# GpSimd's rope sum done head by head, each half with its own count for TensorE's query turn, in an attention and mixture-of-experts layer on one core

## What is computed

```python
norm_q = rmsnorm(x @ W_cq, q_scale)                       # 128 wide
q_nope = (norm_q @ W_dq_nope).reshape(B, S, NH, NOPE)
q_rope = apply_rope((norm_q @ W_dq_rope).reshape(B, S, NH, ROPE), cos, sin)
norm_kv = rmsnorm(x @ W_ckv, kv_scale)                    # 64 wide
scores = concat(q_nope, q_rope) @ concat(k_nope, k_rope / NH) / sqrt(192)
attn = softmax(causal(scores))
x = x + (attn @ value) @ W_o + experts(xn)
```

## Time and profile before

| | |
|---|---|
| median of 3 runs | 1901.81 us (1901.77 to 1904.15) |
| profiled execution | 1908.06 us, span 1906.3 us |
| TensorE busy (PE) | 1479.5 us, 78% |
| VectorE busy (DVE) | 1075.6 us, 56% |
| ScalarE busy (ACT) | 939.0 us, 49% |
| GpSimd busy (POOL) | 647.1 us, 34% |

### The profile page before, as it was taken

The page is one execution under the profiler, slowest core; times in us unless marked ns, Lnnn a source line. Parts: engine busy times, 40 slices in busy tenths (PEclk is TensorE's granted clock), DMA queues, the critical chain, the costliest instruction groups (busy, mean ns, idle before and its releaser), DMA issues. The chain is left out here.

```text
span 1906.3 us, 37123 instructions
## 1 busy us (share of the span) xinstructions
PE 1479.5 (78%) x10111; PEld 1259.3 (66%) x10113; DVE 1075.6 (56%) x4271; ACT 939.0 (49%) x2739; POOL 647.1 (34%) x704
## 2 busy tenths in 40 slices
PE   3662499979799898989989985889998887886340
PEld 2551477767677777777777774678887776775330
DVE  2895266555566555555656653645555666564465
ACT  1330276656566566655666652456666545452000
POOL 1110144434444444444544440000001333334665
PEclk8666699999999999999999997789999889896575
DMA  3992511321311111111111114745455566565553
GB/s 142 341 376 84 226 54 54 127 64 51 143 54 56 53 45 55 61 56 55 41 58 56 46 34 148 248 148 163 150 162 164 182 190 188 181 194 160 158 163 115
DMA packets 169549, 240.44 MB, mean 126 GB/s; under 512 B 16787, under 2 KB 142739, under 8 KB 165011
## 3 DMA queue, kind: packets, MB, share of 16 engines
q1 hardware_dynamic: 146322, 183.61, 29.2%
q0 software_dynamic: 18432, 50.36, 8.5%
q10 hardware_dynamic: 4608, 4.20, 0.8%
HBM read 115.42 MB, written 122.68 MB: 125 GB/s over the span
## 5 line engine op out<-in xcount | busy, mean ns | idle before, releaser
L997 ACT ACTIVATE prob<-prob,negmax 128x512 f32<-128x512 f32 (+3 forms) x512 | 285.5, 560 | 293.4 <-DVE negmax L1073 202.8
L1073 DVE CUSTOM_DVE_ANT_0 prob<-ps,mask_add 128x512 f32<-128x512 f32 (+3 forms) x512 | 248.6, 486 | 240.6 <-issue 237.6
L809 POOL TENSOR_TENSOR qp<-qa,qb 128x512 f32<-128x512 f32 x64 | 81.2, 1269 | 462.5 <-DVE qb L1058 462.5
L61 PE MATMUL ps<-kt_hi,qt_hi 128*128 (+4 forms) x512 | 189.0, 369 | 23.0 <-issue 21.5
L821 POOL DMA_INDIRECT sorted_x<-xn_row,row_no x192 | 188.2, 980 | 48.7 <-issue 44.0
L63 PE MATMUL ps<-kt_hi,qt_lo 128*128 (+4 forms) x512 | 166.8, 326 | 0.0
L62 PE MATMUL ps<-kt_lo,qt_hi 128*128 (+4 forms) x512 | 166.2, 325 | 0.0
L919 PE MATMUL ps<-ident,prob 128*128 128x128 f32 x1280 | 160.7, 273 | 0.0
L935 PE MATMUL ps<-pt,nkv 128*64 128x512 f32 (+3 forms) x1024 | 152.0, 439 | 2.3 <-DVE lat L1091 2.3
L919 PEld LDWEIGHTS ps<-ident,prob 128*128 128x128 f32 x1280 | 143.5, 140 | 0.2 <-ACT prob L997 0.2
L1010 ACT ACTIVATE pt<-ps 128x1024 f32<-128x1024 f32 (+2 forms) x130 | 130.4, 1003 | 14.2 <-PE ps L919 8.7
(11 more groups left out here) (240 smaller groups left out, 4551.4 us busy)
## 6 DMA issues: line engine op xcount, KB each, us to landing
sorted_x<-zeros SPq DMA_DIRECT2D x16, 2048.0 KB, 9.4
rows_in<-sorted_x SPq DMA_DIRECT2D x128, 256.0 KB, 2.8
sorted_y<-rows_out SPq DMA_DIRECT2D x128, 256.0 KB
nqt<-nqt_dram SPq DMA_DIRECT2D x16, 512.0 KB, 3.7
raw_gu<-in_wgu SPq DMA_DIRECT2D x16, 384.0 KB, 4.0
x_in<-in_x SPq DMA_DIRECT2D x8, 512.0 KB, 4.2
xn_dram<-xn SPq DMA_DIRECT2D x8, 512.0 KB, 5.0
xnt_dram<-xnt_hi SPq DMA_DIRECT2D x16, 256.0 KB, 4.7
```

Of the source, the lines that this page charges most:

```text
L61: pe.matmul(out, lh, rh, start=first, stop=False, **kw)
L997: act.activation(prob[:, i, qt, 0:w], prob[:, i, qt, 0:w], ACT.Exp, bias=negmax[:, i, qt:qt + 1], scale=-1.0, accum_out=rowsum[:, g // 2 % ...
L1073: dve.tensor_tensor_reduce(prob[:, i, qt, 0:w], s_ps[k % 2][:, 0:w], mask[:, S - w:S], -1.0, -MASKED, ALU.add, ALU.min, negmax[:, i, qt:qt ...
```

## The change

GpSimd's rope sum of a pair, one instruction over both heads, becomes two, one for each head, and each adds one to `q_done`. TensorE's query turn no longer waits once for the pair; it waits ahead of each head's four transposes for that head's count. Each sum covers 256 elements per partition in place of 512. The wait for `q_abs` stays as it is.

```diff
             def rope_add(b, p):
 
                 pool.wait_ge(q_rope, NP_ * b + p + 1)
-                pool.tensor_tensor(qp[:, :, :, KVR:P], qa[:], qb[:], ALU.add).then_inc(q_done, 1)
+                for i in range(2):
+                    pool.tensor_tensor(qp[:, :, i, KVR:P], qa[:, :, i, :], qb[:, :, i, :], ALU.add)\
+                        .then_inc(q_done, 1)
...
                 pe.wait_ge(q_abs, NP_ * b + p + 1)
-                pe.wait_ge(q_done, NP_ * b + p + 1)
                 for i in range(2):
+                    pe.wait_ge(q_done, NH * b + 2 * p + i + 1)
                     for t in range(TT):
                         mm = pe.transpose(qt_ps[i][:, t * P:(t + 1) * P], qp[:, t, i, :], ident[:])
                     mm.then_inc(qt_ready, 1)
```

## The result

The changed kernel takes 1880.1 us in the median (1875.0 to 1882.0, 4 runs) against 1902.7 (1901.8 to 1904.2, 4 runs) of the kernel before: ratio 0.9876, 95% interval 0.9855 to 0.9898, 22.6 us. The forecast was 12.4 us. The profiled executions differ by more than the medians, 1906.3 to 1879.5 us of span, since the one of the kernel before, 1908.1 us, lay 3.9 us above the highest of its other runs.

The account below looks back on a forecast made before the run. The loop of TensorE's scores, VectorE's chain, GpSimd's sum and the turn was taken to bound the heads stage: 49 x 0.30 = 14.7 us gained, 15 x 0.15 = 2.3 lost, 12.4 net, so 1889.4 us, range 1880 to 1900.

Parts of the forecast that it names:

- (a): GpSimd's rope sum: each half takes 0.73 us, the second ending 1.42 after the sum's start instead of 1.27.
- T: The start of GpSimd's rope sum in a pair, from which the prediction counts its times.
- d: Time the split adds to GpSimd's sum: 0.15 us, with ends at 0 and 0.31.
- The other rule that the prediction weighed: VectorE operations with two SBUF inputs and GpSimd operations exclude each other; the second half reaches 0.15 us further beside VectorE.
- (b): TensorE's query turn: head 0's transposes lie beside GpSimd's second half, so what follows head 1 comes 0.30 us earlier.
- g: Gain per turn from the earlier head 1, 0.45 - d = 0.30 us, in 49 turns.
- (c): Other queues: GpSimd's spread, ScalarE's copies and VectorE's next maximum stay covered, VectorE's idle time shrinking from 1.09 to about 0.8.
- (d): First output pieces: TensorE waits for GpSimd's latent remainder, so 15 of 64 pairs gain nothing and lose 0.15 us each.
- the loop's jumps: Fifth rival: TensorE's gaps there, 7.67 to 1.74 us, can move a few us either way; no separate chance given.
- overlap: First rival: GpSimd's halves overlap, d is 0 to 0.05, gain 18.9 to 22 us, 1880 to 1883; chance 0.08.
- other wait: Third rival: another engine holds TensorE; 1896.8 with half the gain given back, 1902 to 1904 with all; chance 0.14.

Follow-up runs that it names:

- split alone: Changed kernel, but TensorE waits for both halves of the sum before head 0 (also called the kernel with the single wait); ratio 1.0033 to the kernel before.
- swapped waits: Kernel before with only the order of TensorE's waits for `q_abs` and `q_done` ahead of the turn changed, `q_done` first; ratio 0.9967 to the kernel before.
- padded one: Changed kernel with five identity transposes that nobody reads between head 0's and head 1's transposes; ratio 0.9967 to the kernel before.

## Why the prediction was short

The loop that bounds the kernel, VectorE's chain, GpSimd's sum and the turn, was the right one: the plain pairs of the changed kernel, of the split alone and of the swapped waits close on it within 0.01 us once the terms are known, and shortening its next term brought 0.50 a pair more.

(a) held: a half takes 0.730 us (0.73), the second starts 0.69 behind the first, the second ends at T + 1.42, so d = 0.15. The split alone showed it in the pairs with a first piece. That the Trainium skill's GPSIMD Engine Reference, section 2.1, lets a core go on to the next instruction when its share is done gave no more than the 0.04 of overlap that the row had shown; the forecast by the row was right to the hundredth. The other rule that the prediction weighed, on VectorE operations with two SBUF inputs, was not tested: the copy beside the sums reads PSUM alone and the latent product PSUM and one tile in SBUF, so neither is of that kind, and the even times of the sums say nothing on it.

(b) held but for a small term that was mis-sized. TensorE's reaction to the sum, 0.14, was taken from the row of before and carried over to the wait for head 1. In the changed kernel it is 0.05 there, because that wait stands alone ahead of its instruction. That a separate wait costs this much was shown by the swap of two lines. With 0.06 less for it, the gain g of a turn is 0.36, and 40 pairs would bring 14.4 us in place of 12.0 (measured 14.2).

(c) held: VectorE's idle time before the next maximum is 0.74 (about 0.8), and no other engine came up. Two of the prediction's figures were misworked, without weight for the forecast: by its own terms head 0 comes 1.41 - 0.87 = 0.54 us earlier, not 0.57, and d = 0.22 gives 8.0 us, not 7.6.

(d) held: the pairs with a first piece lose 0.14 (0.15), the wait has its row in the trace after, and moving the remainder took it away.

The step that failed is the one on the loop's jumps. I called them a few us either way, which only widened the range, and put them at nothing in the sum beyond their pairs' own share. They and the stage's start brought 10.9 us where the sum had 2.4, of it 6.9 at the four short jumps, where the four pairs' own share is 4 x 0.36 = 1.4. The mean granted clock of the stage, 0.98, hid it, and the first matmul behind the gap doesn't tell: the earlier trace rows gives it 0.79 us at the first jump and 0.50 at the last, but the level behind the last was low as well. The window of the kernel before that begins 0.5 us behind that restart shows it:

```profile
972.52:975.52 3.00, 3.00 (x15) 2.86 (x14) 0.91 (x4) 0.82 (x2) 0.00 (x0) 0.51 0.15 38
```

Such windows behind the jumps could have been read before the forecast. Before and after differ by 1.72 us a short jump, of which 0.36 is the pair. The level there went with the loop's length; the idle time in the turns, the wait in the last turn ahead and the divided wait didn't decide it. Why it goes with the length stays open. For the start, filling the idle time did as much as the change, 2 to 3 us. The long jumps gave 0.9 each; their gaps alone vary between 5.8 and 7.7 us from one to the next and from trace to trace, and that stays open.

Of the rivals, overlap gave nearly the right time (1880 to 1883) for a wrong reason, since d was 0.15 and not 0 to 0.05. No other wait took the place.

## What to carry to other kernels

When one loop sets the time, write its terms from the rows until they close, then divide the producer that stands in it only as far as the consumer can use: here the gain was the consumer's half, not the producer's. Look at what the same queue does further on, since the added instruction delayed another wait in every fourth pair, and at the granted clock behind every gap, window by window, since a change that shortens a loop can move stretches between the two levels.

## What was not expected of the hardware

Where two waits stand ahead of TensorE's first transpose and the one for the later event is a separate sequencer instruction of 51 ns, the first weight load follows that event by 0.11 us in place of 0.05. In the kernel before the order of the two lines decides which wait this is, and it is worth 0.06 us a pair; in the kernel with the single wait the separate instruction is there in 15 of 64 turns only, and exactly these turns are the late ones.

The granted clock behind loop jumps with gaps of about 2 us is at 1.2 GHz for some 3.4 us in 34 of 40 cases in loops with pairs of 12.50 us and more, in 7 of 32 in loops with pairs up to 12.25. Neither the gap's length alone nor TensorE's idle time in the turns tells the two apart. In the kernel before and in the padded one the four stretches at 1.2 GHz begin 116.05 or 116.06 us apart, where the distances of the restarts range from 115.47 to 116.09 us, so the moment of the fall isn't set by the restart.
